# Sparse node sums in stores of 125 destinations, sets turned by transposes, and sums apart added by VectorE

## Chip, cores and metric

One Trainium2 chip (trn2), one NeuronCore of it. The metric is the device time of one execution in microseconds (us), given as the median of the runs. The trace is one profiled execution on that core.

## What is computed

A graph network of two layers on 6250 nodes with 96 features and 106250 edges, sorted by destination `dst`. Cut to what matters:

```python
h   = gelu(x @ W_pre + b_pre)
agg = segment_sum(h[src] * edge_attr, dst)              # layer 0: one 96-wide factor per edge
y   = gelu(gelu((x + agg) @ W1 + b1) @ W2 + b2)
x2  = layernorm(x + (x + agg) + y)
deg = segment_sum(1, dst);  dinv = rsqrt(max(deg, 1))
t   = x2 @ W_lin.T + b_lin
agg2 = segment_sum(t[src] * dinv[src] * dinv[dst], dst)  # layer 1: scalar factors only
out = layernorm(x2 + relu(agg2 + x2 @ W_root.T + b_root))
```

## The kernel before, in words

**Layer 0, the edges.** The edges run in 166 units of 640 (5 tiles of 128) and one last unit of 10. GpSimd (POOL) gathers the source rows of each tile with one indirect DMA (line 848, 791 of them behind 40 early ones at line 827). VectorE (DVE) builds a one-hot matrix of the destinations relative to the group's first one (`onehot`, line 1211, `WIN` = 128 columns) and multiplies the gathered rows by the edge rows (`msg`, line 1227). TensorE (PE) multiplies the two into `seg` (line 1416, two fp32 matmul instructions for a tile). Three units make a group up to unit 155, from unit 156 on each unit is a group; `add` (line 1245) adds a group's `seg` to the turned sums `sumT` (97 rows, one column for each node).

**Layer 0, the nodes.** `step_0` takes the nodes in 14 chunks (`FINE`, the last three of two tiles of 128 nodes) through 16 phases: `colsT` (line 1054), a product (line 1491), transposes (line 1499), a second product, layer norm, turned rows (line 1510), the two products of layer 1 (lines 1376 and 1518), and then `parts`: the rows `t` split into three bf16 parts (lines 1104 to 1109), with the root term written back to `sumT` (line 1116).

**Layer 1 has scalar factors only**, so its sum is a product of a count matrix (how many edges from source s to destination n) with `t`. The count matrix is made from one-hot matrices: for each window of `WD` = 5 destinations, `hots` on DVE (lines 1320, 1322), a matmul for each of the two windows of a pair (line 1447) into PSUM, and a ScalarE (ACT) copy to bf16 (line 935, `keep_pair`). Twelve pairs make a store of `GD` = 120 destinations, and SP sends each store to `counts_hbm` (53 stores). Two stores make a span of `DN` = 240 destinations (27 spans, the last of 10). For each span and each chunk of sources a piece is loaded back to SBUF (eight buffers, `load_piece`), and `sum_piece` multiplies it on PE: three matmuls (line 1476) for each tile of 128 sources, `parts` as weights (96 columns) and the counts as moving data (240 columns). Consecutive pieces of a span form a run in one of three PSUM banks; `dense` (line 1342) adds a run's sum to `sumT`. A span from `SPLIT` = 12 on may be summed before its nodes' root term stands in `sumT`; such a sum is kept apart in `upper` (line 1340), and a later run of the same span takes it up: PE multiplies it by the identity into the bank first (line 1463).

**The last stage.** `step_1` goes over 11 sets of up to five stores (`SETS`). `turn_set` turns `sumT` back to rows of nodes in PSUM (line 1538: a product with the identity, two fp32 instructions for a store); `add_counts` (line 1558) adds the last source tiles, with the counts as weights (120 columns). DVE applies relu, adds `x2` (loaded by `load_back`, lines 744 and 746) and takes statistics (lines 1129 to 1135), POOL and ACT work out the deviation, DVE inverts it (lines 1139, 1141), ACT scales and shifts (line 973, one instruction for a store), and SP stores the set (line 769, and line 771 for the ten last nodes).

**The order** of all engines comes from one list that `schedule()` writes before the run. A unit is followed by what is due: an `add`, `dense`, stores, and then up to 16 tiles of pieces for a unit (`CREDIT`), between pairs and phases of `step_0`. A span can be picked when both its stores are out and its chunk is known; with no span to pick, a unit has no pieces. Each engine runs its part of the list strictly in order. PE waits for `msg` at each unit; a new run waits for the `dense` of the run before it in its bank; `dense` waits for PE's last matmul of the run.

The 14 node chunks end behind the units 25, 40, 53 and so on to 140 (chunk 9), 152 (chunk 10), 159 (chunk 11) and 163 (chunk 12), before and after alike; chunk 13 follows unit 166. Printed from `schedule()`, with the constants of the kernel before and with those of the change:

```
                                          before   change
pieces / matmuls of line 1476                339/3735  313/3453
  of them with 10 columns (span 26)              141       0
runs / runs that take up a sum apart          145/13    138/12
tiles of pieces behind units 0 to 134            881     815
tiles behind units 135 to 151                    128     112
tiles behind units 152 to 165                    230     224
tiles behind unit 166                              6       0
takes among the runs behind units 152 to 166       5       5
dense items behind the last add                    3       0
```

## Time and profile before

| | |
|---|---|
| median of 3 runs | 1154.52 us (1154.5 to 1157.65) |
| the profiled execution | 1157.35 us, span 1155.6 us |
| mean granted TensorE clock | 0.92 |

| engine | busy us | share of the span |
|---|---|---|
| PE | 949.2 | 82% |
| PE weight load | 827.9 | 72% |
| DVE | 726.4 | 63% |
| ACT | 482.0 | 42% |
| POOL | 841.6 | 73% |

Times are us unless marked ns. A row of a timeline starts with the start and the length; a bracket at its end gives how long the engine had been idle and what ended that. Matmuls are pipelined: the length of a row of matmuls holds a tail of some 0.17 us beyond the start of the next, so a pace is read from start to start. The chain that ended last has PE with 42%, POOL 27%, DVE 11%.

### The profile page before, as it was taken

To read this page: it belongs to the slowest core of one execution; us is meant where nothing else is said; L and a number is where in the kernel's file an instruction comes from. 1 tells how busy PE (TensorE), PEld (TensorE's weight loads), DVE (VectorE), ACT (ScalarE), POOL (GpSimd) and SP (SyncE) were. 2 spreads that over 40 slices of the span, in tenths; PEclk is the share of its full clock that TensorE was granted. 3 is DMA by queue.
4 is the path that set the end of the run, shared out by engine and by line. 5 is a ranking of instruction groups with operands and counts; after the bars stand their busy time and mean duration, and the time that the engine had idled before them with its cause. 6 is when DMAs were issued, how large, how long until landed. Compare 5 with 4: busy or idle time off the path is not lost.

```text
span 1155.6 us, 21617 instructions
## 1 busy us (share of the span) xinstructions
PE 949.2 (82%) x7839; PEld 827.9 (72%) x7839; DVE 726.4 (63%) x1409; ACT 482.0 (42%) x825; POOL 841.6 (73%) x922
## 2 busy tenths in 40 slices
PE   6745766767677867888988999989999899799896
PEld 6743544454455846776878888889999799699896
DVE  8177977777677677677676766734335543535655
ACT  2303866656565675565655666520000000101116
POOL 7787777777777777777777777777777777777313
PEclk9876989878768989998999999999999999699998
DMA  8632877566666687878898899889889788488633
GB/s 223 158 113 61 299 261 245 186 199 227 190 205 197 228 292 255 258 261 289 270 281 280 272 291 329 282 282 272 262 254 264 234 225 245 115 245 218 165 80 92
DMA packets 191922, 262.99 MB, mean 228 GB/s; under 512 B 70370, under 2 KB 169698, under 8 KB 184834
## 3 DMA queue, kind: packets, MB, share of 16 engines
q1 hardware_dynamic: 164528, 218.27, 58.9%
q0 software_dynamic: 26992, 42.82, 15.1%
q8 instruction: 66, 1.08, 0.4%
q10 hardware_dynamic: 290, 0.45, 0.2%
q14 instruction: 46, 0.38, 0.1%
HBM read 174.44 MB, written 87.00 MB: 226 GB/s over the span
## 4 chain that ended last, share of the span: by engine, by line
PE 42%; POOL 27%; DVE 11%; issue 11%; DMA 4%; ACT 3%; DVEq 1%; SPq 0%; ACTq 0%; POOLq 0%
PE bank_q L1476 25%; POOL gath L848 23%; PE seg L1416 7%; DMA gath<-table_h,srcs 3%; POOL gath L827 3%; DVE hots_raw L1322 3%; ACT counts_raw L935 2%; PE bank_q L1447 2%; DVE hots_raw L1320 1%; PE bank_q L1558 1%; DVE msg L1227 1%; PE bank_b L1447 1%; PE bank_a L1376 1%; DVE onehot L1211 1%; PE seg L1558 1%
## 5 line engine op out<-in xcount | busy, mean ns | idle before, releaser
L848 POOL DMA_INDIRECT gath<-table_h,srcs x791 | 782.5, 989 | 241.1 <-issue 236.8
L1476 PE MATMUL bank_q<-piece_raw,early_late 128*96 128x240 bf16 (+1 forms) x3735 | 408.2, 264 | 5.7 <-DVE sumT L1342 2.6
L1476 PEld LDWEIGHTS bank_q<-piece_raw,early_late 128*96 128x96 bf16 x3735 | 382.7, 124 | 11.0 <-DVE sumT L1342 3.0
L935 ACT CAST counts_raw<-bank_q 128x490 bf16<-128x490 f32 x417 | 274.9, 708 | 156.7 <-PE bank_q L1447 151.3
L1416 PE MATMUL seg<-onehot,msg 128*97 128x128 f32 x1662 | 240.3, 298 | 76.8 <-DVE msg L1227 50.1
L1416 PEld LDWEIGHTS seg<-onehot,msg 128*97 128x97 f32 x1662 | 216.0, 183 | 94.9 <-issue 64.4
L1447 PE MATMUL bank_q<-hots_raw 128*128 128x245 bf16 x834 | 160.2, 286 | 48.3 <-ACT counts_raw L935 36.7
L1227 DVE TENSOR_TENSOR msg<-gath,edg 128x480 f32<-128x480 f32 x166 | 108.1, 651 | 127.2 <-DMA gath<-table_h,srcs 114.3
L935 ACT CAST counts_raw<-bank_b 128x490 bf16<-128x490 f32 x208 | 147.5, 709 | 91.0 <-PE bank_b L1447 90.4
L1322 DVE TENSOR_TENSOR hots_raw<-counters,kb 128x1960 bf16<-128x1960 bf16 (+1 forms) x157 | 182.2, 1160 | 0.0
L1447 PEld LDWEIGHTS bank_q<-hots_raw 128*128 128x128 bf16 x834 | 71.1, 102 | 108.3 <-ACT counts_raw L935 70.8
L1211 DVE TENSOR_TENSOR onehot<-counters,rel 128x640 f32<-128x640 f32 x166 | 134.5, 810 | 0.0
L1320 DVE TENSOR_TENSOR hots_raw<-counters,kb 128x1024 bf16<-128x1024 bf16 (+1 forms) x157 | 106.4, 678 | 17.3 <-PE bank_q L1447 10.2
L1342 DVE TENSOR_TENSOR sumT<-sumT,bank_q 96x240 f32<-96x240 f32 x107 | 42.7, 399 | 114.7 <-PE bank_q L1476 109.9
L1447 PE MATMUL bank_b<-hots_raw 128*128 128x245 bf16 x416 | 85.6, 289 | 22.5 <-ACT counts_raw L935 15.1
L945 ACT ACTIVATE y<-bank_a,b1c 96x512 f32<-96x512 f32 (+2 forms) x14 | 8.8, 630 | 223.6 <-PE bank_a L1491 223.5
L1447 PEld LDWEIGHTS bank_b<-hots_raw 128*128 128x128 bf16 x416 | 35.2, 103 | 53.6 <-ACT counts_raw L935 33.9
L827 POOL DMA_INDIRECT gath<-in_x,srcs x40 | 38.8, 971 | 12.9 <-issue 11.9
L1245 DVE TENSOR_TENSOR sumT<-sumT,seg 97x128 f32 x62 | 17.6, 283 | 31.9 <-PE seg L1416 24.9
L859 POOL TENSOR_TENSOR gap<-bns 120x5 f32<-120x5 f32 (+1 forms) x11 | 2.2, 199 | 48.3 <-DVE bns L1135 48.2
L1340 DVE COPY upper<-bank_q 96x240 f32<-96x240 f32 (+1 forms) x15 | 5.8, 387 | 41.7 <-PE bank_q L1476 41.6
L1342 DVE TENSOR_TENSOR upper<-upper,bank_q 96x240 f32<-96x240 f32 (+1 forms) x23 | 8.5, 368 | 33.6 <-PE bank_q L1476 33.4
(190 smaller groups left out, 627.5 us busy)
## 6 DMA issues: line engine op xcount, KB each, us to landing
counts_hbm<-counts_raw SPq DMA_DIRECT2D x53, 1470.0 KB
piece_raw<-counts_hbm SPq DMA_DIRECT2D x260, 240.0 KB
edg<-in_edge SPq DMA_DIRECT2D x166, 240.0 KB
gath<-table_h,srcs POOLq DMA_INDIRECT x791
piece_raw<-counts_hbm SPq DMA_DIRECT2D x50, 120.0 KB
piece_raw<-counts_hbm SPq DMA_DIRECT2D x26, 180.0 KB
counts_raw<-counts_hbm SPq DMA_DIRECT2D x4, 600.0 KB, 6.2
table_h<-stage SPq DMA_DIRECT2D x12, 192.0 KB, 2.8
```

The source lines that it names most:

```text
L827: pool.indirect_dma_start(gath[:, t, :], None, x, bass.IndirectOffsetOnAxis(ap=srcs[:, t:t + 1], axis=0)).then_inc(s_xrows[t // CT], 16)
L848: pool.indirect_dma_start(gath[0:k, u % GS * UT + j, :], None, table[0], bass.IndirectOffsetOnAxis(ap=srcs[0:k, t:t + 1], axis=0)).then_in ...
L935: act.copy(counts[:, k % 2, :, i * 2 * WD:(i + 1) * 2 * WD].rearrange("p a (w n) -> p w a n", w=2), pair_bank(m)[:, 0:2 * KC].rearrange("p ...
L1211: dve.tensor_tensor(onehot[:, s], iota_ps[:].unsqueeze(1).to_broadcast([P, UT, WIN]), rel[:, u * UT:(u + 1) * UT].unsqueeze(2).to_broadcas ...
L1227: dve.tensor_tensor(msg[:, s, :, 0:D], gath[:, slot_tiles(u), :], edg[:, u % ES], ALU.mult).then_inc(s_msg, 1)
L1320: dve.tensor_tensor(hot_b(j)[:, 0:n], iota_b.unsqueeze(1).to_broadcast([P, n, P, 2]), blocks.unsqueeze(2).to_broadcast([P, n, P, 2]), ALU. ...
L1322: dve.tensor_tensor(hot_k(j)[:, 0:n], iota_k.unsqueeze(1).to_broadcast([P, n, KC, 2]), keys.unsqueeze(2).to_broadcast([P, n, KC, 2]), ALU. ...
L1342: dve.tensor_tensor(total, total, run_sum, ALU.add).then_inc(s_dense, 1)
L1416: last = pe.matmul(seg[g % 2][0:D + 1, 0:WIN], msg[0:k, u % MS, j, :], onehot[0:k, u % MS, j, :], start=(u == first_unit(g) and j == 0), s ...
L1447: last = pe.matmul(pair_bank(m)[:, w * KC:(w + 1) * KC], hot_b(j)[:, i, :, w], hot_k(j)[:, i, :, w], start=True, stop=True)
L1476: mm = pe.matmul(sums(r)[0:D, 0:n], parts[:, FINE[c] + i, part, :], rows, start=(first and runs[r][3] is None and i == 0 and part == 0), s ...
L1558: last = pe.matmul(set_bank(c)[0:m, t * (D + 1):t * (D + 1) + D], last_counts[c][:, t, (i - first) * GD:(i - first) * GD + m], parts[:, i, ...
```

## The change

A store holds 25 windows, 125 destinations, so there are 50 stores and 25 spans of 250, all full, and 10 sets of five stores. A pair of windows can lie across two stores; ACT then copies its halves apart. `turn_set` uses the transpose mode of TensorE. A run that takes up a sum apart no longer has it multiplied into its bank: `dense` first adds `upper` to `sumT` on DVE. Sets are loaded with one DMA of 125 partitions and stored with two, of 112 and of 13 partitions. In the groups of one unit (units 156 to 166) `onehot`, the matmuls into `seg` and the `add` span 64 columns instead of 128, with the check on the inputs widened for that. Turning any set now waits for the last `add`. An `add` also waits for the `colsT` that stand before it on its own engine.

```diff
+NARROW = 64
-GP = 12
-GD = GP * 2 * WD
-STORES = -(-PAIRS // GP)
+GW = 25
+GD = GW * WD
+STORES = N_NODES // GD
-SPANS = -(-N_NODES // DN)
+SPANS = N_NODES // DN
-SETS = (0, 5, 10, 15, 20, 24, 29, 34, 39, 44, 49, 53)
+SETS = (0, 5, 10, 15, 20, 25, 30, 35, 40, 45, 50)
+ROWS = (slice(0, GD // 16 * 16), slice(GD // 16 * 16, GD))
-LOADED = (0, 1, 2, 3, 7, 4, 5, 6, 10)
+LOADED = (0, 1, 2, 3, 7, 4, 5, 6)
+def reach(g):
+    return WIN if g < WIDE else NARROW
+def last_pair_of(k):
+    return (k * GW + GW - 1) // 2
...
                 # load_back
-                rows, whole, short = by_rows(x2_hbm, c)
-                sp.dma_start(back(c)[:, 0:whole], rows).then_inc(s_back[c % GS], 16)
-                if short is not None:
-                    sp.dma_start(back(c)[0:SHORT, whole, :], short).then_inc(s_back[c % GS], 16)
+                sp.dma_start(back(c), by_rows(x2_hbm, c)).then_inc(s_back[c % GS], 16)
...
                 if p == 7:
                     sp.wait_ge(s_y, n + 1)
-                    rows, whole, short = by_rows(out, c)
-                    sp.dma_start(rows, z[0:GD, c % ZS, 0:whole]).then_inc(s_out[c % ZS], 16)
-                    if short is not None:
-                        sp.dma_start(short, z[0:SHORT, c % ZS, whole, :]).then_inc(s_out[c % ZS], 16)
+                    rows = by_rows(out, c)
+                    for part in ROWS:
+                        sp.dma_start(rows[part], z[part, c % ZS, 0:tiles_in(c, SETS)]).then_inc(s_out[c % ZS], 16)
...
             def keep_pair(m):
+                counted = pair_bank(m)[:, 0:2 * KC].rearrange("p (w a n) -> p w a n", w=2, n=WD)
+                (k, i), (k_last, _) = divmod(2 * m, GW), divmod(2 * m + 1, GW)
...
+                if k_last == k:
+                    act.copy(counts[:, k % 2, :, i * WD:(i + 2) * WD].rearrange("p a (w n) -> p w a n", w=2), counted
+                             ).then_inc(s_kept, 1)
+                else:
+                    act.copy(counts[:, k % 2, :, i * WD:], counted[:, 0])
+                    act.copy(counts[:, k_last % 2, :, 0:WD], counted[:, 1]).then_inc(s_kept, 1)
...
-            dve.tensor_reduce(extent[:, 0:1], rel[:], AX.X, ALU.max)
+            dve.tensor_reduce(extent[:, 0:1], rel[:, 0:WIDE_COLS], AX.X, ALU.max)
+            dve.tensor_reduce(extent[:, 6:7], rel[:, WIDE_COLS:COLS], AX.X, ALU.max)
...
+                w = reach(group_of(u))
                 if u < UNITS:
                     dve.tensor_tensor(
-                        onehot[:, s], iota_ps[:].unsqueeze(1).to_broadcast([P, UT, WIN]),
-                        rel[:, u * UT:(u + 1) * UT].unsqueeze(2).to_broadcast([P, UT, WIN]),
+                        onehot[:, s, :, 0:w], iota_ps[:, 0:w].unsqueeze(1).to_broadcast([P, UT, w]),
+                        rel[:, u * UT:(u + 1) * UT].unsqueeze(2).to_broadcast([P, UT, w]),
                         ALU.is_equal).then_inc(s_oh, 1)
...
+                if before(("add", g), "step0", 0) > 0:
+                    dve.wait_ge(s_x1, before(("add", g), "step0", 0))
...
-                dve.tensor_tensor(sumT[:, bass.ds(b, WIN)], sumT[:, bass.ds(b, WIN)],
-                                  seg[g % 2][0:D + 1, 0:WIN], ALU.add).then_inc(s_add, 1)
+                w = reach(g)
+                dve.tensor_tensor(sumT[:, bass.ds(b, w)], sumT[:, bass.ds(b, w)],
+                                  seg[g % 2][0:D + 1, 0:w], ALU.add).then_inc(s_add, 1)
...
             def dense(r):
...
+                if takes is not None:
+                    dve.tensor_tensor(total, total, high, ALU.add).then_inc(s_taken, 1)
+                    dve.wait_ge(s_taken, sum(1 for v in runs[:r + 1] if v[3] is not None))
+                dve.wait_ge(s_used, q + 1)
...
             def begin_run(r):
...
-                if takes is not None:
-                    pe.wait_ge(s_dense, takes + 1)
-                    pe.matmul(sums(r)[0:D, 0:n], ident[0:D, 0:D],
-                              upper[:, (e - SPLIT) * DN:(e - SPLIT) * DN + n], start=True, stop=False)
...
             def turn_set(n, c):
                 if n < FINALS:
                     pe.wait_ge(s_dense, len(runs))
+                    pe.wait_ge(s_add, GROUPS)
                     pe.wait_ge(s_base, chunks_of(c))
...
                     last = pe.matmul(set_bank(c)[0:GD, t * (D + 1):(t + 1) * (D + 1)],
                                      sumT[:, k * GD:(k + 1) * GD], ident[0:D + 1, 0:D + 1], start=(t == 0),
-                                     stop=(n >= FINALS and t == tiles - 1))
+                                     stop=(n >= FINALS and t == tiles - 1), is_transpose=True)
```

## Rows read from the trace of the kernel before

**Rows 1.** Windows: us, busy us (x instructions) of each engine, PEclk, DMA share, GB/s.

```profile
996.00:1105.00 109.00, 103.78 (x916) 98.78 (x916) 58.03 (x156) 9.94 (x16) 66.60 (x70) 0.94 0.76 200
1105.00:1146.00 41.00, 40.12 (x590) 39.34 (x590) 24.17 (x114) 19.78 (x58) 12.79 (x70) 1.00 0.27 65
```

**Rows 2.** Groups by line on POOL: busy, mean ns, then idle before and its releasers.

```profile
L848 POOL DMA_INDIRECT gath<-table_h,srcs x791 | 782.5, 989 | 241.1 <-issue 236.8 <-DVE msg L1227 4.3
```

**Rows 3.** PE's waits from 755 to 1105 us (us, times, longest), and timeline of PE.

```profile
PE seg L1416 <- DVE msg L1227: 12.2, 5, 4.8
...
996.07 2.42 PE L1416 MATMUL seg<-onehot,msg 128*97 128x128 f32 x10 [3.87 <-DVE msg L1227]
```

**Rows 4.** Timeline of PE, units and pieces; in the second x48, 24 have 10 columns.

```profile
1018.83 1.26 PE L1416 MATMUL seg<-onehot,msg 128*97 128x128 f32 x10
1019.92 5.08 PE L1476 MATMUL bank_q<-piece_raw,early_late 128*96 128x240 bf16 x48
1024.84 1.25 PE L1416 MATMUL seg<-onehot,msg 128*97 128x128 f32 x10
...
1031.94 3.67 PE L1476 MATMUL bank_q<-piece_raw,early_late 128*96 128x240 bf16 x48
1035.47 1.31 PE L1416 MATMUL seg<-onehot,msg 128*97 128x128 f32 x10
```

**Rows 5.** Timeline of PE, one run that takes up a sum apart.

```profile
1060.40 0.57 PE L1463 MATMUL bank_q<-upper,ident 96*96 96x240 f32 x2
1060.81 2.01 PE L1476 MATMUL bank_q<-piece_raw,early_late 128*96 128x240 bf16 x18
```

**Rows 6.** Timeline of PE: transposes of chunk 9, turning of sets 0 and 1.

```profile
914.66 0.50 PE L1499 MATMUL bank_b<-ident,colsT 97*128 97x97 f32 x4
914.99 1.26 PE L1416 MATMUL seg<-onehot,msg 128*97 128x128 f32 x10
...
1105.13 2.34 PE L1538 MATMUL bank_q<-ident,sumT 97*120 97x97 f32 x20 [0.62 <-DVE sumT L1342]
1107.31 0.60 PE L1491 MATMUL bank_a<-colsT,w 96*96 96x256 f32 x2
```

**Rows 7.** Timeline of PE, counts of the last source tiles.

```profile
1116.43 6.75 PE L1558 MATMUL bank_q<-early_late,counts_raw 128*120 128x96 bf16 x120
1123.02 3.46 PE L1558 MATMUL seg<-early_late,counts_raw 128*120 128x96 bf16 x60
```

**Rows 8.** Groups by line on ACT, the copies of the counts from two of three banks.

```profile
L935 ACT CAST counts_raw<-bank_q 128x490 bf16<-128x490 f32 x417 | 274.9, 708 | 156.7 <-PE bank_q L1447 151.3
```

**Rows 9.** Timeline of DVE, before the last stage begins.

```profile
1104.14 0.93 DVE L1342 TENSOR_TENSOR sumT<-sumT,bank_q 96x240 f32<-96x240 f32 x2 [0.15 <-DVE sumT L1342]
1105.00 0.41 DVE L1054 TENSOR_TENSOR colsT<-sumT,xTc 97x256 f32<-97x256 f32 x1
```

**Rows 10.** Timeline of DVE and PE, turned rows of the last chunk.

```profile
1112.49 0.57 DVE L1091 TENSOR_SCALAR xr<-stage,mean,inv 128x96 f32<-128x96 f32 x2 [0.37 <-ACT xr L957]
...
1114.58 0.42 PE L1510 MATMUL bank_b<-ident,xr 128*97 128x128 f32 x2
```

**Rows 11.** Timeline of ACT: first, second and last set scaled and shifted.

```profile
1123.92 1.90 ACT L973 ACTIVATE stage<-stage,shift,inv 120x96 f32<-120x96 f32 x5 [0.46 <-DVE shift L1141]
1126.37 1.90 ACT L973 ACTIVATE stage<-stage,shift,inv 120x96 f32<-120x96 f32 x5 [0.46 <-DVE shift L1141]
...
1149.92 1.54 ACT L973 ACTIVATE stage<-stage,shift,inv 120x96 f32<-120x96 f32 x4 [0.44 <-DVE shift L1141]
```

**Rows 12.** Page of the DMA queues from 1124 to 1144 us: packets, MB, share.

```profile
q1 hardware_dynamic: 4871, 1.82, 38.8%
```

**Rows 13.** Timeline of PE, transposes only, and the window of 1 us behind them.

```profile
95.41 2.39 PE L1428 MATMUL bank_q<-ident,piece_raw 128*128 128x128 f32 x10 [23.05 <-DVE extent L1298]
...
100.00:101.00 1.00, 0.85 (x4) 0.68 0.23 49
```

**Rows 14.** One line's instructions, ns min/median/max: matmuls on every second 2-byte element.

```profile
L1447 PE MATMUL bank_q<-hots_raw x834: 269/273/413, 107.8 to 756.4; 128*128 128x245 bf16 x167
```

More of the change, by code:

```diff
@@ L192, in pick @@
             ready = span_chunk(e) < known or e >= SPLIT
[L193 removed]
+            if ready and stored[2 * e + 1] + 4 <= u:
                 gain = FINE[upto(e)] - FINE[summed[e]]
@@ L238, in schedule @@
                 order.append(("pair", pairs[i]))
-                if pairs[i] == PAIRS - 1 or pairs[i] % GP == GP - 1:
-                    stored[pairs[i] // GP] = u + 1
+                for k in range(STORES):
+                    if last_pair_of(k) == pairs[i]:
+                        stored[k] = u + 1
             if credit >= CT:
@@ L353, in build @@
         onehot = sb("onehot", [P, MS, UT, WIN])
-        rooms = {c: room for room, sets in ((counts_raw[:], (0, 1, 2, 3, 7)), (hots_raw[:], (4, 5, 6, 10)),
+        rooms = {c: room for room, sets in ((counts_raw[:], (0, 1, 2, 3, 7)), (hots_raw[:], (4, 5, 6)),
                                             (edg[:].rearrange("p s j d -> p (s j d)"), (8, 9)))
@@ L562, in out_before @@
         def out_before(n, c):
-            whole = 16 * (len(range(c % ZS, FINALS, ZS)) + (c % ZS == (FINALS - 1) % ZS))
-            return n // FINALS * whole + 16 * (c // ZS)
+            each = 16 * len(ROWS)
+            return each * (n // FINALS * len(range(c % ZS, FINALS, ZS)) + c // ZS)
         def back_count(n, c):
-            whole = len(range(c % GS, FINALS, GS)) + (c % GS == (FINALS - 1) % GS)
-            return 16 * (n // FINALS * whole + c // GS + 1 + (c == FINALS - 1))
+            return 16 * (n // FINALS * len(range(c % GS, FINALS, GS)) + c // GS + 1)
         def x_count(n):
@@ L599, in by_rows @@
         def by_rows(tab, c):
-            nodes = set_nodes(c)
-            whole = (nodes.stop - nodes.start) // GD * GD
-            short = tab[nodes.start + whole:nodes.stop, :] if whole < nodes.stop - nodes.start else None
-            return tab[nodes.start:nodes.start + whole, :].rearrange("(t p) d -> p t d", p=GD), whole // GD, short
-        SHORT = N_NODES % GD
+            return tab[set_nodes(c), :].rearrange("(t p) d -> p t d", p=GD)
         def set_bank(c):
@@ L708, in load_piece @@
                 e, c = pieces[q][:2]
-                stores = range(2 * e, min(2 * e + 2, STORES))
-                for k in stores:
-                    sp.wait_ge(s_store[k % 2], 16 * (k // 2 + 1))
+                for s in range(2):
+                    sp.wait_ge(s_store[s], 16 * (e + 1))
                 if q >= PS:
@@ L714, in load_piece @@
                 cols = slice(FINE[c] * GD, FINE[c + 1] * GD)
-                sp.dma_start(piece[:, q % PS, 0:len(stores), 0:tiles_in(c) * GD],
-                             counts_hbm[stores.start:stores.stop, :, cols].rearrange("h b n -> b h n")
+                sp.dma_start(piece[:, q % PS, :, 0:tiles_in(c) * GD],
+                             counts_hbm[2 * e:2 * e + 2, :, cols].rearrange("h b n -> b h n")
                              ).then_inc(s_piece[q % PS], 16)
@@ L784, in _ @@
                     ahead = min(item[1] + PS, len(pieces))
-                while loaded < ahead and min(2 * pieces[loaded][0] + 2, STORES) <= stores_sent:
+                while loaded < ahead and 2 * pieces[loaded][0] + 2 <= stores_sent:
                     load_piece(loaded)
@@ L1415, in unit @@
                 for j, k in enumerate(sizes(u)):
-                    last = pe.matmul(seg[g % 2][0:D + 1, 0:WIN], msg[0:k, u % MS, j, :], onehot[0:k, u % MS, j, :],
+                    last = pe.matmul(seg[g % 2][0:D + 1, 0:reach(g)], msg[0:k, u % MS, j, :],
+                                     onehot[0:k, u % MS, j, 0:reach(g)],
                                      start=(u == first_unit(g) and j == 0),
@@ L1451, in begin_run @@
             def begin_run(r):
-                e, _, _, takes = runs[r]
-                n = span_end(e) - e * DN
                 if run_before(r) is not None:
@@ L1473, in sum_piece @@
                 for i in range(tiles_in(c)):
-                    rows = piece[:, q % PS, :, i * GD:(i + 1) * GD] if n == DN else piece[:, q % PS, 0, i * GD:i * GD + n]
+                    rows = piece[:, q % PS, :, i * GD:(i + 1) * GD]
                     for part in range(3):
-                        mm = pe.matmul(sums(r)[0:D, 0:n], parts[:, FINE[c] + i, part, :], rows,
-                                       start=(first and runs[r][3] is None and i == 0 and part == 0),
+                        mm = pe.matmul(sums(r)[0:D, 0:DN], parts[:, FINE[c] + i, part, :], rows,
+                                       start=(first and i == 0 and part == 0),
                                        stop=(last and i == tiles_in(c) - 1 and part == 2))
```

64 lines of the change are left out of this document (30 added, 34 removed).

## Prediction

> **What bounds the kernel now.** I read the windows by stage first, then the groups on POOL, then PE's waits, then timelines of PE, DVE and ACT. Three things set the end one after another. POOL gathers without a pause: 791 gathers are 782.5 us busy and 241.1 us between them, of which only 4.3 us is a wait for anybody [rows 2]. It is a clock that no other engine moves, and the change doesn't touch it. Up to 996 us PE follows that clock: it still has 12.2 us of waits for `msg` behind 755 us, the last one at 996.07, 3.87 us long, at unit 151 [rows 3]. Behind that wait PE never catches up again. From 996 to 1105 us it is busy for 103.8 of 109 us, and in the last stage for 40.1 of 41 us [rows 1]. So work taken from PE before 996 us is worth nothing, since POOL's data would then be waited for longer; work taken from it behind unit 151 counts in full. In the last stage ACT has a pace of its own: set 1 follows set 0 after 2.45 us, each time 0.46 us behind DVE's `shift` [rows 11], a loop of ACT, DVE and ACT again. From set 0 to set 10 there are 26.0 us, 2.60 a set [rows 11], so PE's pace there is only a little slower than ACT's.
>
> **Part 1, before unit 151: nothing.** The planner gives 112 tiles of pieces behind units 135 to 151 where there were 128, and 815 instead of 881 before them. With 250 columns for 240 a tile costs about 4% more, so the earlier stretch has 849 of the old tiles in place of 881, the 10-column ones among them. PE comes to unit 151 no later. The counts: 25 of the 625 pairs lie across two stores, and ACT makes two half copies of them. A whole copy takes 708 ns [rows 8], so this is between 0 and 25 x 0.71 = 18 us of ACT, spread over 650 us in which ACT waits for PE for 151 us on two of three banks [rows 8]; PE's 12.2 us of waits for POOL [rows 3] lie behind it. The longer start on DVE (one reduction cut in two, three tiny operations) and the new wait of `add` for `colsT` (its own engine's earlier work) also lie under POOL's clock. Cost nought; if that cover were gone, a few us.
>
> **Part 2, from unit 151 to the last stage.** Pieces: before, 236 tiles, 708 matmuls, of which 36 have 10 columns. 48 matmuls of 240 columns take 1024.84 - 1019.92 = 4.92 us, 0.1025 each; 24 of them and 24 with 10 columns take 3.53 us, so a short one costs (3.53 - 2.46)/24 = 0.045 us, the weight load alone [rows 4]. Together 672 x 0.1025 + 36 x 0.045 = 70.5 us. After, 224 tiles, exactly 672 matmuls. No row has 250 columns; as 240 columns cost more than twice the 0.045 of the weights, columns set the pace, and I take 0.1025 x 250/240 = 0.1068, together 71.7 us. **+1.2 us** (0 to +2): the shorter list was made of short matmuls, and here the change of store size brings no gain.
>
> Sums apart: five runs in this stretch take one up. The pair of fp32 matmuls costs 1060.81 - 1060.40 = 0.41 us of PE [rows 5]: **-2.05 us**. DVE gets an extra addition of 240 columns for each, 0.4 us like those of [rows 9], placed before its wait for PE, and DVE is busy for 58 of 109 us here [rows 1]. Queued behind it are the addition of the run itself and, through it, the bank. If this cover failed the gain would be nought.
>
> Units 156 to 165 with 64 columns: ten matmuls of 128 columns take 1.09 us (1019.92 - 1018.83) [rows 4]. With half the columns the weights may set the pace. Turning shows it: 20 fp32 matmuls with 120 weight columns and 97 moving ones take 2.18 us, 0.109 each [rows 6], although 97 columns at the pace of 128 would be 0.083. Per weight column 0.91 ns, for 97 of them 0.088, a unit 0.88 us: 10 x 0.21 = **-2.1 us**. Bounds: 0, and half of 1.09, -5.4 us. I take the weights, the nearer row. The shorter `onehot` and `add` shorten DVE's part where it is late; I count none of that.
>
> The hand-over: before, three `dense` follow the last `add` and the last 18 matmuls run beside them [rows 9]; after, all `dense` stand ahead of that `add`, and nothing of pieces is left behind unit 166. The wait for the last `add` that every set now has takes their place. About 1 us of PE idle before and after: nought, +-1. The sum of part 2 is +1.2 - 2.05 - 2.1 = **-2.95 us**.
>
> **Part 3, the last stage.** Its start is a chain through the last node chunk, with PE's own work in between. The product at 1107.31 stands behind the turning of two sets, 20 instructions in 2.18 us. A transpose is one instruction for a store: four of 97 columns take 914.99 - 914.66 = 0.33 us, 0.083 each [rows 6]. Ten take 0.83: -1.35 us, and set 2, in front of the second product, gives another 0.3. At the turned rows PE is late by more: DVE has them at 1113.06, PE takes them at 1114.58 [rows 10], and ahead of them stand sets 3 and 4, nine stores at 0.218 against ten at 0.083 (-1.1 us), and the counts of sets 0 and 1, 60 matmuls. Such a one costs (1123.02 - 1116.43)/120 = 0.0549 [rows 7]; with 125 weight columns for 120 I take 0.0572, +0.14. The chain comes 1.35 + 0.3 + 1.1 - 0.15 = 2.6 us earlier, DVE's rows then just in time, and set 0 leaves PE 2.45 us earlier.
>
> What is late next is ACT. PE needs 5 x 0.083 + 30 x 0.0572 = 2.13 us for each of sets 5 to 9, under ACT's 2.45. Nine steps of 2.45 are 22.05 us in place of 26.0: -3.95. Sets 3 and 4 have more counts (60 and 54 matmuls, 3.4 and 3.1 us) and hold ACT up once, +0.55. The last set has five stores for four: 1.90 for 1.54 us [rows 11], +0.36. Two stores of 112 and 13 partitions end it, where two of 120 and 10 did; 200 more rows there, +0.3 by the packet's price below. Sum: -2.45 - 3.95 + 0.55 + 0.36 + 0.3 = **-5.2 us** (-3 to -6.5).
>
> **Sum.** -2.95 - 5.2 = -8.15 us on the profiled execution: 1157.35 - 8.15 = 1149.2. The median lies 2.83 us under the profiled execution, so 1146.4 us.
>
> **Rivals.** (a) **The clock falls in the last stage (slower).** Fewer and lighter instructions could let the granted clock go to 1.2 GHz there. PE's 354 count matmuls and 25 transposes from then on, some 23 us, would double, ACT would wait for PE, and the end would come 22 us later: 1168 us. It turns the result to slower once more than 8.2 us are lost, a bit over a third of the stage. Against it: from 95.41 us PE does nothing but 24 transposes, at the half clock, and in the window of 100 to 101 us the clock rises (0.68) [rows 13]. And in sets 5 to 9 only 0.4 of 2.1 us are transposes. 5%. The Trainium skill, page TensorE: Matmul & The Clock Gate, section Part 4: PE-mode transpose, says that the full clock doesn't engage for transposes, since they don't count as activity; the rows just named speak against that. By that rule the time would be that of this rival; by the trace it is the forecast.
>
> (b) **Odd row starts (slower).** Rows of 125 bf16 counts begin 2 bytes off a word for every second tile. Were PE to read these at a slower pace, 336 matmuls behind unit 151 would carry it; it decides from 8.15/336 = 0.024 us each, and 0.1 us each would give 1180 us. Against it: the 834 count matmuls read each second 2-byte element, from both halves of a word, at 269/273 ns minimum and median for either [rows 14]. 4%.
>
> (c) **The set loads clog five engines.** 4871 packets took 38.8% of 16 engines for 20 us [rows 12], 0.0255 us each. Spread evenly a load of 625 rows is 39 packets an engine, 1.0 us. On five engines it would be 125, 3.2 us. Eight such loads stand behind units 159 to 166, 17.6 us more on these five, which are busy for 76% [rows 1] of some 49 us: 5.8 us too much. Pieces are loaded eight ahead, 15 us of PE's work, so I expect no wait; were it all to come through, 1152.2 us. 6%. The Trainium skill, page DMA: Bandwidth & Descriptors, section on why a DMA increments its semaphore by 16, says that a copy runs on the largest number of engines up to 16 that divides its outer size, five for 125; no row before the change has 125 partitions.
>
> (d) **The gain of part 2 turns into waits** for `dense` and `add`: PE has 5.2 us of idle there now [rows 1]. If these grow by 3 us and half of part 3 is lost to DVE in its loop, about 1152 us. 11%. (e) **The transpose takes two instructions** as the product did: PE then keeps its 2.7 us a set, part 3 gives -2, 1149.6 us. 5%.
>
> **How the numbers follow.** Forecast 69%, (e) 5%, both faster; (d) 11% and (c) 6% within 0.3%, which is about what a measurement of this kernel can tell from no change (3.5 us); (a) 5% and (b) 4% slower. So faster 0.74, same 0.17, slower 0.09. Around the forecast: units at half price give 3.3 us more, part 3 from +2.2 to -1.3, the takes +2, the hand-over +-1. The range runs from 1141 to 1153.5 us, which takes in (c), (d) and (e) and leaves out (a) and (b).
>
> **What would show it.** The wait at unit 151 again near 996 us; the pace of 48 piece matmuls at 5.13 us; a narrow unit at 0.88; turning a set at 0.41 us; ACT's sets 2.45 us apart, the first one near 1118.5 us; granted clock 1.00 in the last stage. It would be wrong if the wait at unit 151 were gone, if PE waited for `piece_raw` from a DMA, or if the pace of pieces were not that of columns.

## The result, and the profile of the changed kernel

The changed kernel takes 1151.4 us, median of 20 (1146.1 to 1153.5), beside 1154.8 us, median of 20 (1152.8 to 1157.9), of the kernel before: a ratio of 0.9957, 95% interval 0.9946 to 0.9968, or 3.7 to 6.2 us. It is faster: by 5.0 us from the ratio, where 8.1 were forecast (1154.5 to 1146.4), or 3.5 us from the two medians. The 20 times lie in two groups with nothing between 1149.4 and 1151.1: eight at 1147.7 us in the mean and twelve at 1152.2. The forecast of 1146.4 is nearer to the lower group. The profiled execution is of the upper one: 1152.15 us, span 1150.4.

Windows of the changed kernel: PE is again busy for 103 of 109 us up to 1105, but then the granted clock is 0.87 where it was 1.00 [rows 1]. About 0.08 of the missing 0.13 is a fall up to 1111.7 us; the rest is half clock from 1142.4 us on, when PE has done its last matmul and nothing waits for it.

```profile
996.00:1105.00 109.00, 103.31 (x896) 99.28 (x895) 57.28 (x165) 11.69 (x19) 65.78 (x68) 0.94 0.76 202
1105.00:1146.00 41.00, 33.91 (x485) 33.45 (x484) 23.11 (x108) 20.43 (x63) 12.82 (x70) 0.87 0.28 68
...
1099.00:1101.00 2.00, 1.21 (x11) 1.24 (x12) 0.65 (x2) 0.00 (x0) 0.00 (x0) 1.00 0.73 185
1102.00:1111.00 9.00, 9.00 (x70) 9.00 (x69) 2.74 (x16) 1.94 (x5) 0.00 (x0) 0.50 0.12 29
1112.00:1140.00 28.00, 26.91 (x422) 26.45 (x420) 19.14 (x85) 15.27 (x46) 11.54 (x63) 1.00 0.31 75
```

From 1102 to 1111 us the clock is at half, 1.2 GHz. PE is busy without a gap in it; the gap lies ahead, at the hand-over to the last stage. Timeline of PE in the changed kernel (start, duration, line, tiles, count; in brackets the idle time before and what ended it):

```profile
994.49 2.42 PE L1439 MATMUL seg<-onehot,msg 128*97 128x128 f32 x10 [5.07 <-DVE msg L1243]
...
1013.82 5.32 PE L1493 MATMUL bank_q<-piece_raw,early_late 128*96 128x250 bf16 x48
1018.98 1.25 PE L1439 MATMUL seg<-onehot,msg 128*97 128x128 f32 x10
...
1031.48 0.99 PE L1439 MATMUL seg<-onehot,msg 128*97 128x64 f32 x10
1032.31 1.88 PE L1493 MATMUL bank_q<-piece_raw,early_late 128*96 128x250 bf16 x16
...
1098.03 0.38 PE L1439 MATMUL seg<-onehot,msg 10*97 10x64 f32 x2
1099.79 1.30 PE L1554 MATMUL bank_q<-ident,sumT 97*125 97x97 f32 x10 [1.38 <-DVE sumT L1365]
1100.92 0.60 PE L1508 MATMUL bank_a<-colsT,w 96*96 96x256 f32 x2
1101.36 0.40 PE L1516 MATMUL bank_b<-ident,colsT 97*128 97x97 f32 x2
...
1103.46 2.31 PE L1554 MATMUL seg<-ident,sumT 97*125 97x97 f32 x10
1105.57 6.44 PE L1574 MATMUL bank_q<-early_late,counts_raw 128*125 128x96 bf16 x60
1111.85 0.42 PE L1527 MATMUL bank_b<-ident,xr 128*97 128x128 f32 x2
```

The wait at unit 151 (994.49) answers to rows 3, the 48 matmuls and the units of 128 and 64 columns to rows 4, the turning to rows 6. At full clock ten transposes take 1100.92 - 1099.79 = 1.13 us; the ten from 1103.46 take 2.11. The 60 counts behind them take 1111.85 - 1105.57 = 6.28 us; at full clock 60 of them take 3.47 (the next 120 need 6.93).

Timeline of DVE in the changed kernel, before the last stage (rows 9):

```profile
1097.91 0.41 DVE L1365 TENSOR_TENSOR sumT<-sumT,bank_q 96x250 f32<-96x250 f32 x1 [0.20 <-DVE sumT L1365]
1098.52 0.41 DVE L1365 TENSOR_TENSOR sumT<-sumT,bank_q 96x250 f32<-96x250 f32 x1 [0.20 <-DVE sumT L1365]
1099.46 0.22 DVE L1264 TENSOR_TENSOR sumT<-sumT,seg 97x64 f32 x1 [0.53 <-DVE sumT L1365]
1099.72 0.42 DVE L1064 TENSOR_TENSOR colsT<-sumT,xTc 97x256 f32<-97x256 f32 x1
```

The last unit's addition stands behind all additions of runs, with 0.53 us of idle DVE ahead of it. Timeline of ACT in the changed kernel, sets 0, 2, 3, 7, 8 and 9 scaled and shifted (rows 11), and one wait of DVE:

```profile
1121.35 1.90 ACT L983 ACTIVATE stage<-stage,shift,inv 125x96 f32<-125x96 f32 x5 [0.46 <-DVE shift L1151]
...
1126.29 1.90 ACT L983 ACTIVATE stage<-stage,shift,inv 125x96 f32<-125x96 f32 x5 [0.50 <-DVE shift L1151]
1129.42 1.90 ACT L983 ACTIVATE stage<-stage,shift,inv 125x96 f32<-125x96 f32 x5 [1.13 <-DVE shift L1151]
...
1139.27 1.90 ACT L983 ACTIVATE stage<-stage,shift,inv 125x96 f32<-125x96 f32 x5 [0.49 <-DVE shift L1151]
1142.29 1.90 ACT L983 ACTIVATE stage<-stage,shift,inv 125x96 f32<-125x96 f32 x5 [1.02 <-DVE shift L1151]
1144.74 1.90 ACT L983 ACTIVATE stage<-stage,shift,inv 125x96 f32<-125x96 f32 x5 [0.45 <-DVE shift L1151]
...
1140.30 0.16 DVE L1139 TENSOR_SCALAR eps_degs<-bank_q 125x5 f32<-125x5 f32 x1 [1.06 <-DMA out_y<-stage]
```

Most sets follow one another after 2.45 to 2.49 us; set 3 after 3.13, and set 8 after 3.02, because DVE waits 1.06 us for a store that still reads the buffer it wants.

The two profiled executions, cut at the same five points:

| stretch | before | changed | difference | forecast |
|---|---|---|---|---|
| to unit 151's sum | 996.07 | 994.49 | -1.58 | 0 |
| to the first turning | 109.06 | 105.30 | -3.76 | -2.95 |
| to set 0's z on ACT | 18.79 | 21.56 | +2.77 | -2.45 |
| to the last set's z | 26.00 | 23.39 | -2.61 | -3.40 |
| last set | 1.54 | 1.90 | +0.36 | +0.36 |
| to the end of the span | 4.14 | 3.76 | -0.38 | +0.3 |

The sum is -5.2 us for a forecast of -8.15. One row carries the miss: the third, 5.2 us worse than forecast. The first row, -1.58 for nothing, is POOL's and no work of the change.

### The profile page after: what moved, and what is told of

Same layout as the page of the kernel before. It is cut to its first block and busy times, and to the rows that moved or that the text cites. A ratio compares the mean times of both kernels' runs of the same rounds, so it can differ in the third digit from the quotient of the medians.

```text
span 1150.4 us, 20771 instructions
## 1 busy us (share of the span) xinstructions
PE 939.1 (82%) x7455; PEld 818.7 (71%) x7455; DVE 724.1 (63%) x1410; ACT 499.1 (43%) x846; POOL 838.7 (73%) x915
## 5 line engine op out<-in xcount | busy, mean ns | idle before, releaser
L854 POOL DMA_INDIRECT gath<-table_h,srcs x791 | 780.8, 987 | 241.1 <-issue 239.6
L1493 PE MATMUL bank_q<-piece_raw,early_late 128*96 128x250 bf16 x3453 | 403.1, 271 | 5.1 <-ACT counts_raw L943 2.7
L1493 PEld LDWEIGHTS bank_q<-piece_raw,early_late 128*96 128x96 bf16 x3453 | 377.6, 123 | 8.7 <-DVE sumT L1365 2.9
L943 ACT CAST counts_raw<-bank_q 128x490 bf16<-128x490 f32 x400 | 279.7, 757 | 152.1 <-PE bank_q L1471 148.5
L1439 PE MATMUL seg<-onehot,msg 128*97 128x128 f32 (+1 forms) x1662 | 239.2, 298 | 77.0 <-DVE msg L1243 54.3
L1471 PE MATMUL bank_q<-hots_raw 128*128 128x245 bf16 x834 | 159.5, 287 | 49.5 <-ACT counts_raw L943 35.3
L943 ACT CAST counts_raw<-bank_b 128x490 bf16<-128x490 f32 x200 | 151.5, 757 | 69.9 <-PE bank_b L1471 67.2
L1227 DVE TENSOR_TENSOR onehot<-counters,rel 128x640 f32<-128x640 f32 (+1 forms) x166 | 131.3, 791 | 0.0
L1365 DVE TENSOR_TENSOR sumT<-sumT,bank_q 96x250 f32<-96x250 f32 x105 | 43.1, 410 | 126.2 <-PE bank_q L1493 120.2
L1264 DVE TENSOR_TENSOR sumT<-sumT,seg 97x128 f32 (+1 forms) x62 | 16.9, 272 | 33.9 <-PE seg L1439 28.2
L1363 DVE COPY upper<-bank_q 96x250 f32<-96x250 f32 x13 | 5.4, 415 | 44.8 <-PE bank_q L1493 44.8
L1365 DVE TENSOR_TENSOR upper<-upper,bank_q 96x250 f32<-96x250 f32 x20 | 8.2, 410 | 40.2 <-PE bank_q L1493 40.2
```

Source lines behind the costliest of these rows:

```text
L854: pool.indirect_dma_start(gath[0:k, u % GS * UT + j, :], None, table[0], bass.IndirectOffsetOnAxis(ap=srcs[0:k, t:t + 1], axis=0)).then_in ...
L943: act.copy(counts[:, k % 2, :, i * WD:(i + 2) * WD].rearrange("p a (w n) -> p w a n", w=2), counted).then_inc(s_kept, 1)
L1227: dve.tensor_tensor(onehot[:, s, :, 0:w], iota_ps[:, 0:w].unsqueeze(1).to_broadcast([P, UT, w]), rel[:, u * UT:(u + 1) * UT].unsqueeze(2). ...
L1365: dve.tensor_tensor(total, total, run_sum, ALU.add).then_inc(s_dense, 1)
L1439: last = pe.matmul(seg[g % 2][0:D + 1, 0:reach(g)], msg[0:k, u % MS, j, :], onehot[0:k, u % MS, j, 0:reach(g)], start=(u == first_unit(g) ...
L1471: last = pe.matmul(pair_bank(m)[:, w * KC:(w + 1) * KC], hot_b(j)[:, i, :, w], hot_k(j)[:, i, :, w], start=True, stop=True)
```

## Experiments

Three theories on the half clock and the two groups. **Theory 1**: the idle time at the hand-over, 1.38 us for 0.62 [rows 6], sometimes makes the clock fall. **Theory 2**: the transposes do, rival (a). **Theory 3**: the groups are POOL's luck and the fall is in all executions.

The first four kernels ran on one chip, beside 22 runs of the kernel before with a median of 1155.9 us (1152.7 to 1159.3).

**The changed kernel again.**

> The changed kernel once more, so that the others have it on the same chip. Its profile had TensorE's granted clock at 0.50 from about 1101.7 to 1111.4 us, behind 1.4 us without a matmul and 15 transposes; its 20 times lie in two groups, 1146.1 to 1149.4 and 1151.1 to 1153.5. If the clock's fall makes the groups, executions near 1147 have no such stretch and those near 1152 have one. If the groups come from elsewhere (POOL, a DMA), the fall is in both.

Measured: 1149.7 us, median of 8 (1147.0 to 1153.4), ratio 0.9949 (0.9930 to 0.9968). Its profiled execution, 1151.6 us, again has 1.38 us of idle PE at the hand-over, then half clock from 1101.2 to 1111.5. So the fall repeats; whether it is absent from the low times this profile can't say. The two groups don't repeat as clearly: one of the eight times, 1150.07, lies in the gap between them. The mean granted clock of each execution helps only in part. In the first 20 it is 0.916 for the lower group and 0.909 for the upper, the way of a fall. In these eight it doesn't sort the times, and the execution with the profiled fall has the highest of them, 0.918.

**Products for transposes, in the changed kernel.**

```
-    stop=(n >= FINALS and t == tiles - 1), is_transpose=True)
+    stop=(n >= FINALS and t == tiles - 1))
```

> The changed kernel, with the sets turned by products with the identity as before, not by transposes. Theory 1, the fall comes from the 1.4 us in which TensorE has nothing at the hand-over to the last stage: that idle time is still there, the clock falls again, and the time is 1152 to 1155 us. Theory 2, transposes don't count as work for the clock: it stays at 1.00, and with 50 products of two instructions (about 0.2 us each against 0.113) on a path that only partly shows them, the time is 1147 to 1150 us.

Measured: 1153.6 us, median of 10, ratio 0.9988 (0.9963 to 1.0012). There are two groups here too, five at 1149.0 to 1150.7 and five at 1156.5 to 1159.9. The profiled execution is of the lower one (1150.1 us): idle as before, and no fall. Windows and timeline of PE, and two sets on ACT, of the kernel with products:

```profile
1097.00:1099.00 2.00, 1.11 (x10) 1.14 (x11) 0.68 (x3) 0.00 (x0) 0.00 (x0) 1.00 0.74 189
1100.00:1110.00 10.00, 9.54 (x114) 9.06 (x114) 3.43 (x19) 2.76 (x6) 0.00 (x0) 1.00 0.12 30
...
1097.89 1.30 PE L1554 MATMUL bank_q<-ident,sumT 97*125 97x97 f32 x10 [1.38 <-DVE sumT L1365]
...
1131.19 1.90 ACT L983 ACTIVATE stage<-stage,shift,inv 125x96 f32<-125x96 f32 x5 [0.85 <-DVE shift L1151]
1134.05 1.90 ACT L983 ACTIVATE stage<-stage,shift,inv 125x96 f32<-125x96 f32 x5 [0.86 <-DVE shift L1151]
```

The two groups without any transpose in the sets speak against theory 2, but no profile is of the upper one, which lies 7 us above the lower where the changed kernel's lies 4.5. Theory 1 survives in a weaker form: the same idle time is followed by a fall in some executions and not in others. With products the sets 4 to 7 come 2.86 us apart, PE's pace, for 2.45. The interval of this kernel takes in 1: by the times, the change without its transposes isn't shown to be faster.

**Transposes alone, in the kernel before.** The same edit the other way round.

> The kernel before, with the sets turned by transposes and nothing else changed. Its hand-over has only 0.6 us without a matmul. Theory 1 (idle time): the clock stays at 1.00 and the transposes give 2 to 4 us: 1151 to 1153 us. Theory 2 (transposes don't count): the clock falls behind 1105 us as in the changed kernel, and the time is that of before or longer, 1154 to 1158 us. A transpose is expected at 0.11 us for 0.109 x 2 of a product.

Measured: 1151.2 us, median of 7 (1147.6 to 1153.2), ratio 0.9962 (0.9945 to 0.9980): 4.4 us less by the ratio (2.3 to 6.4), where 2 to 4 were expected. The whole change gives 5.9 us on this chip (e1: 3.7 to 8.1). The intervals overlap, so by the times most of the gain is this one part, and the gain of the rest isn't clear of noise. Windows of the kernel before with transposes, from its first turning on:

```profile
1103.00:1113.00 10.00, 9.33 (x125) 8.69 (x126) 4.93 (x24) 2.75 (x6) 0.00 (x0) 1.00 0.08 22
1113.00:1138.00 25.00, 24.13 (x416) 23.79 (x414) 18.89 (x87) 15.43 (x47) 11.56 (x63) 1.00 0.39 89
```

The idle time is 0.62 us and the clock stays at 1.00 with all transposes in place. Set 0's z comes 15.94 us behind the first turning, for 18.79, and the sets take 24.59 us for 26.00. So transposes alone don't bring the fall, and theory 2 falls. The Trainium skill says on the page TensorE: Matmul & The Clock Gate, section Part 4: PE-mode transpose, that transposes don't count as activity for the full clock; this trace doesn't agree, with 53 transposes at a clock of 1.00. What is left of theory 2 is that it takes both, the idle time and transposes behind it. That isn't excluded at this place, as the only profile with 1.38 us and products has no fall; it isn't so everywhere, since the kernel before has a fall with no set turned near it (below, at 1080 us).

**The idle time filled.** Thirteen matmuls into a bank that nobody reads, ahead of the first transpose.

```
+    if n == 0:
+        pe.wait_ge(s_t, CUTS - 1)
+        pe.wait_ge(s_base, CUTS - 1)
+        for _ in range(13):
+            pe.matmul(bank_a[0:D, 0:DN], parts[:, 0, 0, :], ..., start=True, stop=True)
```

> The changed kernel with 13 matmuls of 250 columns into a bank that nobody reads (some 1.4 us at full clock), between the last unit's sum and the first transpose, where TensorE waits. Theory 1 (idle time): the clock stays at 1.00 in every execution, and the time is 1146 to 1148 us, with one group in place of two. Theory 2 (transposes): the clock falls behind them as before, 1151 to 1153 us.

Measured: 1147.2 us, median of 6 (1145.5 to 1150.4), ratio 0.9931 (0.9911 to 0.9952). Windows, timeline of PE and first set on ACT of the kernel with the filler:

```profile
1102.00:1111.00 9.00, 8.54 (x106) 8.05 (x105) 3.57 (x19) 2.75 (x6) 0.00 (x0) 1.00 0.33 86
1112.00:1137.00 25.00, 24.28 (x392) 24.15 (x390) 17.53 (x83) 14.18 (x43) 10.51 (x58) 1.00 0.35 84
...
1099.61 0.38 PE L1440 MATMUL seg<-onehot,msg 10*97 10x64 f32 x2
1099.92 1.59 PE L1545 MATMUL bank_a<-early_late 128*96 128x250 bf16 x13
1101.38 1.30 PE L1561 MATMUL bank_q<-ident,sumT 97*125 97x97 f32 x10
...
1118.25 1.90 ACT L984 ACTIVATE stage<-stage,shift,inv 125x96 f32<-125x96 f32 x5 [0.46 <-DVE shift L1152]
```

With the same transposes and no idle time the clock stays at 1.00, and set 0's z comes 1118.25 - 1101.38 = 16.87 us behind the first turning, for 21.56 in the changed kernel: the fall costs 4.7 us, and the two groups' means are 4.5 apart. None of six times reaches the upper group, which holds 12 of 20 and 3 of 8 of the changed kernel's. But one group was expected, at 1146 to 1148, and the six are three at 1145.5 to 1145.8 and three at 1148.7 to 1150.4. The median is 2.5 us under e1's with intervals that overlap, so the times alone don't show the filler's gain. This profiled execution, 1149.2 us, has no fall: its unit 151 was summed at 996.80, 2.3 us after the changed kernel's. So theory 3 has its share: POOL moves the end by some 3 us (unit 151 is summed at 993.7 to 996.8 in these four traces and the first two), the clock by 4.7.

Counted from unit 151's sum to the end of the span, which takes POOL's part out, the six profiles have 159.5 us (before), 155.9 (changed), 154.6 (e1), 154.5 (e2), 155.4 (e3) and 150.6 (e4). The filler kernel is 4.0 us shorter than e1 here. The transposes alone give 4.1 us for the kernel before, and the change with the filler 8.9, where 8.15 were forecast for an execution without a fall.

On the three chips that the other eight kernels met, every kernel had a median of 1611 us or more, the one before as well (1628, 1649 and 1627), and a ratio's interval is +-6 us or wider. Why was not settled. In e9's trace the gathers are as long as ever (768.9 us), but POOL idles 703.8 us between them for 241.1, 486.6 of it waiting for DVE's `msg` (1.5 in the changed kernel). These times can't tell 0.3%, and I draw nothing from them; from 50 us before the end on, the traces run at their usual pace, and these stretches I use.

**The last unit ahead of the last two pieces**, to leave as little as possible late at the hand-over.

```
+    last = [("unit", UNITS), ("back", GS - 1), ("add", GROUPS - 1)]
+    order = [x for x in order if x not in last]
+    at = order.index(("piece", len(pieces) - 2))
+    order[at:at] = last
```

> The changed kernel with the last unit's sum and its addition moved ahead of the last two pieces. All that TensorE then waits for at the hand-over is the last run's addition, as in the kernel before: 0.6 us idle for 1.38. Theory 1 (the clock falls because of the idle time, whatever follows): 1.00 from 1096 to 1135 us in the profile, one group of times around 1146.5, none above 1150. Theory 3 (POOL's luck alone makes the two groups): two groups, 1147 and 1152, as before.

> The same order, with the sets turned by products in place of transposes. In the changed kernel products gave two groups, 1149.0 to 1150.7 and 1156.5 to 1159.9. Theory 1 (idle time): with the short idle time only the lower group is left, 1149 to 1150 us. Theory 2 (transposes' missing activity): then the products would never have had a high group, and nothing here is different from e2.

Measured: ratios 1.0031 (0.9886 to 1.0177) and 0.9988 (0.9938 to 1.0038), too wide for either theory. In both profiles the idle time is 0.99 us, not the 0.6 expected, and no half clock follows. Timeline of PE in e5:

```profile
1578.30 1.83 PE L1499 MATMUL bank_q<-piece_raw,early_late 128*96 128x250 bf16 x12
1581.12 1.33 PE L1560 MATMUL bank_q<-ident,sumT 97*125 97x97 f32 x10 [1.00 <-DVE sumT L1371]
```

Set 0's z stands 16.9 us behind the first turning in e5 and 19.6 in e6, as in e4 and e2.

**Transposes of 128 columns for 125**, on top of that order. Only 125 of the 128 partitions that they write are read.

```
-    pe.matmul(set_bank(c)[0:GD, ...], sumT[:, k * GD:(k + 1) * GD], ...
+    pe.matmul(set_bank(c)[:, ...], sumT[:, k * GD:k * GD + P], ...
```

> The same order, and the transposes read 128 columns of sumT and write 128 partitions (three more than are used). Transposes with 128 weight columns took 0.083 us each elsewhere in the traces, those with 125 take 0.113. If the number of weight columns makes the difference, ten of them take 0.83 us for 1.13, the first z comes 0.7 us earlier and the time is 0.7 us less than e5. If it is the fp32 operand sumT or its address, nothing changes.

> The changed kernel with the last unit ahead of the last two pieces (idle time at the hand-over 1.0 for 1.4 us) and with transposes that read and write 128 columns and partitions (0.087 for 0.113 us each). Theory 1, idle time makes the clock fall: no half clock between 1095 and 1130 us, one group of times near 1145.5, 0.991 to 0.993 of before. If groups stay that lie 4 to 5 us apart, the fall has another cause.

> The same kernel as e9 once more, on another chip, to have its time beside a before of 1155 us: theory 1 (idle time at the hand-over makes the clock fall) has one group of times, 1144.5 to 1148 us, 0.992 of before. Theory 3 (POOL's luck makes the groups) has two, 4 to 5 us apart.

Measured in time: ratios 0.9884 (0.9796 to 0.9972), 0.9904 (0.9866 to 0.9942) and 0.9984 (0.9949 to 1.0020) for one and the same kernel. They show how little these chips can tell; that this kernel beats the changed one is not shown, and e9's and e11's question, one group or two, stays open. Timeline of PE in e9:

```profile
1589.24 1.05 PE L1560 MATMUL bank_q<-ident,sumT 97*128 97x97 f32 x10 [0.99 <-DVE sumT L1371]
1590.13 0.60 PE L1514 MATMUL bank_a<-colsT,w 96*96 96x256 f32 x2
```

Ten transposes take 0.89 us for 1.13: three more columns make them 0.024 us shorter each. Clock 1.00 behind 0.99 us of idle time in all three profiles, and z at 16.4 us behind the first turning, 0.55 us earlier than in e5 where 0.7 were expected. But it isn't that more columns are quicker. The transposes of e3 have 120 weight columns and are as quick as these. Timeline of PE in e3:

```profile
1103.21 1.05 PE L1538 MATMUL bank_q<-ident,sumT 97*120 97x97 f32 x10 [0.62 <-DVE sumT L1342]
1104.09 0.60 PE L1491 MATMUL bank_a<-colsT,w 96*96 96x256 f32 x2
```

Ten take 0.88 us with 120, 1.13 with 125 and 0.89 with 128; from start to start inside a row it is 0.083, 0.109 and 0.083 us. Of the three, 125 alone is slow, by 0.026 us a transpose, and that is the size of store which the change chose. Why is open.

**Windows of 128 columns for all units**, on top of both (NARROW = 128).

> The same with windows of 128 columns for all units, as before the change. A unit of ten matmuls costs 1.09 us for 0.83: ten units on TensorE's path, +2.6 us against e9, and nothing else differs. If VectorE or POOL set the pace of this stretch, +0.

Measured: 0.9958 (0.9919 to 0.9998) beside e9's 0.9904, 1644.3 for 1636.6 us: the sign is the expected one, the size is lost in the spread. The trace has the price. Timeline of PE in e10, then in e9, the same unit:

```profile
1592.83 1.30 PE L1445 MATMUL seg<-onehot,msg 128*97 128x128 f32 x10
1593.97 5.32 PE L1499 MATMUL bank_q<-piece_raw,early_late 128*96 128x250 bf16 x48
```

```profile
1577.27 0.99 PE L1445 MATMUL seg<-onehot,msg 128*97 128x64 f32 x10
1578.09 5.32 PE L1499 MATMUL bank_q<-piece_raw,early_late 128*96 128x250 bf16 x48
```

1.14 us for 0.82: 0.32 us a unit here, and 1.09 - 0.83 = 0.26 between the kernel before and the changed one.

**The sums apart taken up by PE again**, on top of the order (e8) and of both (e12).

```
-    dve.tensor_tensor(total, total, high, ALU.add).then_inc(s_taken, 1)
+    pe.matmul(sums(r)[0:D, 0:DN], ident[0:D, 0:D], upper[...], start=True, stop=False)
```

> The same order, with the sums apart taken up by TensorE again, two fp32 matmuls of 0.41 us together, and VectorE's extra addition gone. If the prediction's cover holds, TensorE needs 2.05 us more from unit 151 to the last stage: e5 + 2. If VectorE's addition (0.61 us with the gap behind it) was on the path as well, the two cancel: e5 + 0 to 1.

> The same with the sums apart taken up by TensorE (0.41 us each, five behind unit 151) and without VectorE's extra addition. By the prediction +2.05 us against e11; if VectorE's additions are on the path as well, 0 to +1. The idle time at the hand-over was 1.35 us here on another chip, with the clock at half behind it, so a second group 4 to 5 us higher is expected by theory 1.

Measured: e8 1618.8 us, a median of four without a ratio, e12 0.9939 (0.9903 to 0.9975) beside e11's 0.9984. The sign is not the expected one, and the intervals overlap: the +2.05 us is neither shown nor refuted. What the traces add is the hand-over: 1.35 us of idle PE in both; in e8 the clock is at 0.50 from 1560 to 1569 us behind it, and in e12 it isn't. Set 0's z stands 21.64 us behind the first turning in e8, for 16.92 in e5, which has the same transposes: the price of a fall is 4.7 us once more. Windows of e8:

```profile
1558.00:1559.00 1.00, 0.51 (x5) 0.52 (x5) 0.75 (x2) 0.00 (x0) 0.00 (x0) 1.00 1.16 283
1559.00:1560.00 1.00, 1.00 (x9) 1.00 (x8) 0.00 (x0) 0.00 (x0) 0.00 (x0) 0.76 0.97 253
1560.00:1561.00 1.00, 1.00 (x5) 0.65 (x4) 0.00 (x0) 0.12 (x1) 0.00 (x0) 0.50 0.24 62
```

**All fourteen profiles together.** With 1.35 to 1.38 us of idle PE at the hand-over: a fall in three (the changed kernel, e1, e8), none in two (e2, e12). With 0 to 1.0 us: none in nine (before, e3 to e7, e9 to e11), eight of them without e4's filler. Of the eleven with transposes three have a fall. So at this place a fall goes with the longer idle time. The length alone doesn't decide: the same 1.35 to 1.38 us are followed by a fall or by none. Earlier in the traces there is a wait of 1.74 or 1.75 us for `dense`, in all twelve profiles of the changed kernel and its variants, and never a fall right behind it. The kernel before and e3 have 1.81 us there, and a fall both times. What decides stays open.

## Why the prediction was right or wrong

**The sign and the range were right, the likeliest time was 5 us too low.** The median lies in the range, in its upper part, and that is partly luck: the upper part was there for rivals (c), (d) and (e), and the one rival with a falling clock stood outside it, at 1168 us. 1146.4 was forecast for an execution without a fall. If the lower group is those, they lie at 1147.7. Of the signs named, the clock of 1.00 in the last stage and set 0 near 1118.5 us failed (0.50 for 10 us, and 1121.35), and a set takes 0.56 us to turn for 0.41.

**The bound: right.** The wait at unit 151 is there again, 5.07 us, 1.58 us earlier; e1 to e4 have it at 993.7 to 996.8 us, for either kernel. So nothing before it counts. ACT's copies of counts grew from 708 to 757 ns without a trace in the end.

**Part 2: -3.76 us for -2.95, with errors that partly cancel.** Pieces: 48 matmuls in 5.16 us, 0.1075 each, for 0.1068. A narrow unit 0.83 us for 0.88, so -2.6 for -2.1 us: half the columns don't halve the time (that would be 0.55), as the weights were said to set the pace, and it is a little faster than rows 6 had it. Takes: the 0.41 us left PE, and PE's waits for the bank within the stretch are 1.74 and 0.69 us, where the kernel before has 1.81 and 0.74; DVE's extra additions are hidden. The hand-over, put at nought, costs +0.76 us. These terms give +1.7 - 2.6 - 2.05 + 0.76 = -2.2. Four others were not in the forecast. The kernel before has a fall at 1080.3 us, in which ten matmuls of a unit and six of a piece take 1.6 us more than at full clock; the changed one hasn't. It also has three short waits before matmuls of units, 1.2 us in all, and the changed one has none. The other way, the half clock behind unit 151 that both have costs the changed kernel 1.1 us more in its first unit and 72 piece matmuls, and PE waits 0.6 us for turned rows. With these the sum is -3.3; half a microsecond stays unassigned. Window of the kernel before, at the start of its fall:

```profile
1080.00:1081.00 1.00, 0.55 (x4) 0.58 (x4) 0.80 (x3) 0.00 (x0) 0.99 (x1) 0.64 0.51 106
```

E3's trace, with the order of before, has it too (0.50 at 1079 to 1081 us, behind 1.81 us of idle PE), and the changed kernel, e1, e2 and e4 have not, behind 1.74 or 1.75 us. I had read these waits, not the clock behind them.

**The step that failed is the hand-over: "nought, +-1".** I saw that every addition of a run stood ahead of the last unit's and that nothing was left for PE, and priced the idle time at itself. The kernel before had 18 matmuls beside the additions of [rows 9], which left it 0.62 us. Timeline of PE in the kernel before:

```profile
1102.46 2.05 PE L1476 MATMUL bank_q<-piece_raw,early_late 128*96 128x240 bf16 x18
```

What follows is dearer than the idle time: half clock over 10 us, among them the 60 counts ahead of the turned rows, 4.7 us in an execution that has it. In twelve of twenty it does, if the upper group is read as those; one of these twelve was profiled, and one of e1's above 1151 us, and both have it; no execution of the lower group was profiled.

**Rival (a) had the right effect and the wrong price, and its cause doesn't hold alone.** It was given 5% and 22 us, with the transposes as cause, and argued away by what transposes do to the clock [rows 13]. That argument held as far as it went (e3, e4). But I asked only what keeps the clock up within the stage, not what makes it fall at its door, and took the fall to last to the end, where it lasts some 10 us.

**Part 3: the mechanism right, one term mis-sized.** A transpose is one instruction, so (e) is out, but it costs 0.113 us at full clock, not 0.083: I took the price of one with 128 weight columns [rows 6] for one with 125. That is 25 x 0.03 = 0.75 us on the way to set 0's z. With the 120 columns of the stores before, the price would have been nearly right (0.088 in e3), so what was missed is the cost of 125 itself. Without the fall this stretch took 16.87 us for a forecast of 16.34. ACT's loop is the pace from then on, as forecast, at 2.45 us. Set 3's extra was 0.68 for 0.55, and set 8's wait for a store, 0.57, I had not seen. It is 0.05 in e1 and nought in e7. Without the transposes PE is the pace again (e2, 2.86 us). Last set +0.36, as forecast; the end 0.38 shorter, not 0.3 longer.

**Rival (c): the mechanism is there, its price is hidden.** In the last stage two loads of 125 partitions run alone; in the kernel before, two of 120. Windows of the changed kernel, then of the kernel before (the last two columns are the DMA share of 16 engines and GB/s):

```profile
1121.00:1122.00 1.00, 1.00 (x21) 1.00 (x20) 0.93 (x5) 0.65 (x2) 0.77 (x5) 1.00 0.37 102
1122.00:1123.00 1.00, 1.00 (x22) 1.00 (x19) 0.89 (x5) 1.00 (x4) 0.39 (x3) 1.00 0.37 102
```

```profile
1122.10:1122.80 0.70, 0.70 (x17) 0.70 (x15) 0.67 (x4) 0.00 (x0) 0.59 (x3) 1.00 0.91 248
```

The changed kernel's loads sit at 0.37 of 16 engines and 102 GB/s, without rise or fall; those of before reach 0.91 and 248 GB/s. So the trace agrees with the Trainium skill, page DMA: Bandwidth & Descriptors, section on why a DMA increments its semaphore by 16, by which 125 rows run on five engines: that would be 0.31, near the 0.37 of the rows. The loads move at less than half of that peak, and nobody is late by it: from 996 us on PE never waits for `piece_raw` from a DMA, nor DVE for `gath` in the last stage. The 6% and the cover named were fair. **Rival (b)** is out by the pace of 0.1075 us with every second tile on an odd start, and **(d)** by the waits named above. **(e)** is the nearest in time, 1149.6 us, and is out by the instruction count.

## What to carry to other kernels

When an edit moves work away from the place where one stage waits for the last result of another, look at what is left for TensorE there: 1.4 us of idle time instead of 0.6 cost up to 4.7 us here, as the clock went to half over 10 us of dense work behind it. A few matmuls into a free bank kept it up in the one profile taken: 150.6 us from unit 151 to the end for 154.6. The medians, 1147.2 for 1149.7 us, lie within the spread. Where a kernel's times fall in two groups, read the granted clock in windows of 1 us before anything else, and profile an execution of each group. Take a duration only from a row with the same number of weight columns: here 125 cost more than both 120 and 128.

## What the runs showed of the hardware

- Ten fp32 transposes with 97 moving columns take 0.88 us with 120 weight columns (e3), 1.13 with 125 (the changed kernel) and 0.89 with 128 (e9), at full clock.
- At the two places compared, one idle time of TensorE of 1.35 to 1.81 us between stretches of dense work was followed by half clock five times and not fourteen times (1.35 to 1.38: three of five; 1.74 to 1.75: none of twelve; 1.81: two of two). At the hand-over, up to 1.0 us it never was, in nine traces. That is no limit: in e10 half clock from 1531.6 us on stands behind gaps of 0.2 to 0.4 us in a row, with PE busy for about half the time.
- Fifty transposes in a stage, five or ten of them back to back at its start, among some 350 other matmuls, leave the clock at 1.00 (e3, e4, e5, e7, e9 to e12).
- Two loads of 125 partitions moved 102 GB/s at a DMA share of 0.37, two of 120 up to 248 GB/s at 0.91.
- The kernel before took 1155 and 1156 us in two measurements and 1627 to 1649 on three other chips. A variant's trace there has equally long gathers (768.9 us) and about three times the idle time between them; the cause is open.
